# Splitting the shared expert's weights on another engine, and the routing weights and slot experts at other places

## The reference, cut to what matters

```python
xt = x.reshape(-1, 256)                                   # 4096 tokens
scores = softmax(xt @ gate_w.T)                           # 8 experts
_, idx = top_k(scores + gate_bias, 2)
weights = take_along_axis(scores, idx, axis=1)
for e in range(8):
    gate_e = sum(where(idx == e, weights, 0.0), axis=1)
    h = silu(xt @ w1[e].T) * (xt @ w3[e].T)
    y = y + gate_e[:, None] * (h @ w2[e].T)
z = silu(xt @ sw1.T) * (xt @ sw3.T) @ sw2.T               # the shared expert, 512 wide
return y + z
```

## Time and profile before

| | |
|---|---|
| median of 3 timed runs | 662.98 us (662.78 to 662.98) |
| profiled execution, time | 657.85 us |
| its span | 656.1 us |
| PE busy | 556.5 us (85%) |
| DVE busy | 467.4 us (71%) |
| ACT busy | 329.1 us (50%) |
| POOL busy | 269.9 us (41%) |
| granted PE clock, mean | 0.936 |

### The profile page before, as it was taken

One profiled execution on the slowest core, in us unless ns is written; L12 is line 12 of the kernel. 1 busy time (PEld: TensorE's weight loads), 2 busy tenths in 40 slices (PEclk: granted clock), 3 DMA queues, 4 the chain that ended last, 5 costly groups with the idle time before them and its releaser, 6 DMA issues.

```text
span 656.1 us, 11544 instructions
## 1 busy us (share of the span) xinstructions
PE 556.5 (85%) x3488; PEld 484.3 (74%) x3488; DVE 467.4 (71%) x1252; ACT 329.1 (50%) x678; POOL 269.9 (41%) x564
## 2 busy tenths in 40 slices
PE   2728899966598997953799999899999999998885
PEld 1727489956567997632788888688888888887764
DVE  4983997888499874568777764566666666665795
ACT  0516998424389870651455443255555555554321
POOL 4061300033223001000677666366667666665680
PEclk9878999969698998987799999999999999999998
DMA  9998000000000001900222222323333333331994
GB/s 275 335 268 3 1 1 1 2 1 0 1 0 1 2 1 58 400 25 0 73 92 83 83 75 91 98 91 101 106 107 107 107 103 109 100 107 65 316 309 144
DMA packets 57130, 63.04 MB, mean 96 GB/s; under 512 B 14736, under 2 KB 50448, under 8 KB 57072
## 3 DMA queue, kind: packets, MB, share of 16 engines
q1 hardware_dynamic: 49216, 43.75, 23.3%
q0 software_dynamic: 6480, 17.90, 7.7%
q10 hardware_dynamic: 1376, 0.66, 0.5%
HBM read 30.64 MB, written 31.65 MB: 95 GB/s over the span
## 4 chain that ended last, share of the span: by engine, by line
PE 51%; DVE 6%; issue 1%; ACT 1%; POOL 0%; DVEq 0%; POOLq 0%
PE bank L1206 15%; PE bank L1208 15%; PE bank L1207 15%; PE bank L1329 2%; PE bank L1345 2%; PE bank L1214 1%; PE bank L1258 1%; DVE h_lo L1136 1%; DVE XN L975 1%; DVE sw_lo L1021 1%; DVE X L1109 0%; DVE mv L972 0%; DVE X L1119 0%; PE bank L1231 0%; ACT sw_hi L890 0%
## 5 line engine op out<-in xcount | busy, mean ns | idle before, releaser
L830 POOL DMA_INDIRECT slots_in<-X,slot x64 | 68.5, 1070 | 86.4 <-DVEq L1093 52.8
L854 POOL DMA_INDIRECT token_out<-YS,to_row x71 | 71.7, 1010 | 54.3 <-DVE back L1173 50.2
L577 PE MATMUL a_bank<-VO,E_hi 128*128 128x258 f32 x272 | 78.1, 287 | 6.9 <-DVE E_lo L484 6.8
L581 PE MATMUL a_bank<-VO,E_lo 128*128 128x258 f32 x272 | 77.5, 285 | 0.0
L579 PE MATMUL a_bank<-VO,E_hi 128*128 128x256 f32 x272 | 77.4, 285 | 0.0
L1162 DVE TENSOR_TENSOR hr<-bank,sr 128x256 f32<-128x256 f32 x71 | 30.1, 425 | 59.4 <-ACT sr L934 59.4
L1206 PE MATMUL bank<-W_hi,XST_hi 128*128 x142 | 61.8, 435 | 0.5 <-DVE XST_lo L1178 0.5
L934 ACT ACTIVATE sr<-bank 128x256 f32<-128x256 f32 x71 | 27.3, 385 | 63.2 <-PE bank L1208 63.2
L1206 PE MATMUL bank<-XT_hi,sw_hi 128*128 128x512 f32 x128 | 52.1, 407 | 7.7 <-DVE XT_lo L1013 6.1
L577 PEld LDWEIGHTS a_bank<-VO,E_hi 128*128 128x128 f32 x272 | 52.2, 192 | 7.8 <-DVE E_lo L484 7.8
L908 ACT ACTIVATE h_hi<-hf 128x512 fp32r<-128x512 f32 x32 | 20.2, 632 | 74.2 <-DVE hf L1128 74.2
(11 more groups left out here) (241 smaller groups left out, 1700.1 us busy)
## 6 DMA issues: line engine op xcount, KB each, us to landing
XS<-slots_in SPq DMA_DIRECT2D x71, 131.0 KB, 2.0
slots_in<-blank SPq DMA_DIRECT2D x7, 1179.0 KB, 14.4
YG<-token_out SPq DMA_DIRECT2D x16, 512.0 KB, 8.7
W_raw<-in_wT_dram SPq DMA_DIRECT2D x8, 768.0 KB, 13.0
X<-in_x_dram SPq DMA_DIRECT2D x8, 512.0 KB, 7.1
out_dram<-X SPq DMA_DIRECT2D x32, 128.0 KB, 1.9
token_out<-YS,to_row POOLq DMA_INDIRECT x71, 2.5
slots_in<-blank SPq DMA_DIRECT2D x1, 1048.0 KB, 14.7
```

The costliest lines, as they stand in the source:

```text
L577: pe.matmul(O_ps[Q % 2][j][:, 0:D + 2], E_hi[:, n % NE, cols], VO[:, kt, 0:D + 2], start=(kt == 0), stop=False)
L581: mm = pe.matmul(O_ps[Q % 2][j][:, 0:D + 2], E_lo[:, n % NE, cols], VO[:, kt, 0:D + 2], start=False, stop=(kt == qt))
L830: pool.indirect_dma_start(out=xs, out_offset=bass.IndirectOffsetOnAxis(ap=slot[k][:, t:t + 1], axis=0), in_=X[:, t, :], in_offset=None).th ...
L854: pool.indirect_dma_start(out=ys, out_offset=bass.IndirectOffsetOnAxis(ap=to_row[:, i:i + 1], axis=0), in_=YS[:, i % NYS, :], in_offset=No ...
```

## The change

Three things are moved, none is removed.

1. The split of the shared weights goes to POOL, all four instructions, behind its constants and as soon as the two loads have landed. ACT loses L889 to L891, DVE L1019 to L1022. PE waits for the new semaphore `s_slo`.
2. The weights of the two choices (5 instructions of DVE) are worked out behind `chosen` and ahead of the wait for the counts. `s_slot` is now counted by each of the two instructions that write `slot[k]`, with no wait behind the second; the scatters of the first group are issued for choice 0 as soon as `slot[0]` is there, and for choice 1 behind `slot[1]`.
3. `slot_experts()` stands in chunk 4 (`n == MC`) instead of chunk 0. Its count of `s_slot` is waited for as 3.

```diff
@@ gpsimd
+            pool.wait_ge(s_w, 32)
+            for w, (raw, hi, lo) in enumerate(((sw13_raw, sw13_hi, sw13_lo), (sw2_raw, sw2_hi, sw2_lo))):
+                pool.tensor_copy(hi[:, :, :], raw[:, :, :]).then_inc(s_shi, 1)
+                pool.wait_ge(s_shi, w + 1)
+                pool.tensor_tensor(lo[:, :, :], raw[:, :, :], hi[:, :, :].bitcast(f32), ALU.subtract)\
+                    .then_inc(s_slo, 1)
...
             pool.wait_ge(s_slot, 1)
-            for t in range(NT):
-                if t % GT == 0 and t > 0:
+            for t in range(GT):
+                scatter(t, 0)
+            pool.wait_ge(s_slot, 2)
+            for t in range(GT):
+                scatter(t, 1)
+            for t in range(GT, NT):
+                if t % GT == 0:
                     pool.wait_ge(s_sc[t // GT - 1], 16 * TOPK * GT)
                 for k in range(TOPK):
-                    pool.indirect_dma_start(out=xs,
...
+                    scatter(t, k)
...
-            pool.wait_ge(s_slot, 2)
+            pool.wait_ge(s_slot, 3)
@@ scalar
             logits_copy(NG - 1, 1)
-            act.wait_ge(s_w, 32)
-            act.activation(sw13_hi[:, :, :], sw13_raw[:, :, :], ACT.Copy).then_inc(s_whi, 1)
-            act.activation(sw2_hi[:, :, :], sw2_raw[:, :, :], ACT.Copy).then_inc(s_whi, 1)
@@ vector
-            dve.wait_ge(s_whi, 3)
-            for raw, hi, lo in ((sw13_raw, sw13_hi, sw13_lo), (sw2_raw, sw2_hi, sw2_lo)):
-                dve.tensor_tensor(lo[:, :, :], raw[:, :, :], hi[:, :, :].bitcast(f32), ALU.subtract)\
-                   .then_inc(s_wlo, 1)
             group_lo(0)
...
+            for k, out in ((1, X[:, :, W1]), (0, X[:, :, DW])):
+                done(dve.tensor_tensor(tmp[:, :, :], pick[k][:, :, :], score[:, :, :], ALU.mult))
+                done(dve.tensor_reduce(out, tmp[:, :, :], AX.X, ALU.add))
+            done(dve.tensor_tensor(X[:, :, DW], X[:, :, DW], X[:, :, W1], ALU.subtract))
+            dve.wait_ge(s_cols, 3)
             dve.wait_ge(s_cnt, 1)
...
-                done(dve.tensor_copy(slot[k][:, :], red[:, :]))
-            for k, out in ((1, X[:, :, W1]), (0, X[:, :, DW])):
...
-            dve.wait_ge(s_cols, 3)
-            dve.sem_inc(s_slot, 1)
+                dve.tensor_copy(slot[k][:, :], red[:, :]).then_inc(s_slot, 1)
...
-                        if n == 0:
+                        if n == MC:
                             slot_experts()
@@ tensor
-            pe.wait_ge(s_wlo, 3)
+            pe.wait_ge(s_slo, 2)
...
-            pe.wait_ge(s_slot, 2)
+            pe.wait_ge(s_slot, 3)
```

More of the change, by code:

```diff
@@ L697, in attention_and_experts @@
         s_wlo = sem("f_wlo")
+        s_shi = sem("f_shi")
+        s_slo = sem("f_slo")
         s_mv = sem("f_mv")
@@ L823, in _, with scatter @@
                                      pattern=[[1, P]], channel_multiplier=-1))
-            pool.wait_ge(s_slot, 1)
-            for t in range(NT):
-                if t % GT == 0 and t > 0:
+            pool.wait_ge(s_w, 32)
[4 more added lines that the diff above has]
+                    .then_inc(s_slo, 1)
+            def scatter(t, k):
+                pool.indirect_dma_start(out=xs,
+                                        out_offset=bass.IndirectOffsetOnAxis(ap=slot[k][:, t:t + 1], axis=0),
+                                        in_=X[:, t, :], in_offset=None).then_inc(s_sc[t // GT], 16)
+            pool.wait_ge(s_slot, 1)
+            for t in range(GT):
[5 more added lines that the diff above has]
+                if t % GT == 0:
                     pool.wait_ge(s_sc[t // GT - 1], 16 * TOPK * GT)
                 for k in range(TOPK):
-                    pool.indirect_dma_start(out=xs,
-                                            out_offset=bass.IndirectOffsetOnAxis(ap=slot[k][:, t:t + 1], axis=0),
-                                            in_=X[:, t, :], in_offset=None).then_inc(s_sc[t // GT], 16)
+                    scatter(t, k)
             def meta_of(i):
@@ L1086, in _ @@
                 done(dve.tensor_reduce(red[:, :], tmp[:, :, :], AX.X, ALU.add))
-                done(dve.tensor_copy(slot[k][:, :], red[:, :]))
-            for k, out in ((1, X[:, :, W1]), (0, X[:, :, DW])):
-                done(dve.tensor_tensor(tmp[:, :, :], pick[k][:, :, :], score[:, :, :], ALU.mult))
-                done(dve.tensor_reduce(out, tmp[:, :, :], AX.X, ALU.add))
-            done(dve.tensor_tensor(X[:, :, DW], X[:, :, DW], X[:, :, W1], ALU.subtract))
-            dve.wait_ge(s_cols, 3)
-            dve.sem_inc(s_slot, 1)
+                dve.tensor_copy(slot[k][:, :], red[:, :]).then_inc(s_slot, 1)
             def slot_experts():
```

## The result

| | before | after |
|---|---|---|
| median of 11 runs each, side by side | 661.18 us (658.10 to 663.78) | 656.05 us (654.51 to 658.01) |
| ratio of the times, 95% interval | | 0.992 (0.9902 to 0.9939) |
| profiled execution, its span | 657.85, 656.1 | 654.51, 652.8 |

The change is worth 5.1 us by the medians, 5.3 by the ratio (4.0 to 6.5 by its interval); 5.5 were forecast. The two profiled executions differ by 3.3 us only, and a good part of this study is about the gap between these two numbers.

A forecast was written before the change was run, and what follows sets the result against it. DVE was taken as the bound from the end of the logits until PE's outputs(0) at 315.13. Savings 4.4 + 0.9 + 1.3 less 1.1 make 5.5 us: median 662.98 to 657.5 us, range 655.7 to 662.2.

The forecast's parts named there:

- Part 1, saved 4.40 us: End of logits: with the split on POOL, group 0's XT_lo ends at 287.97 instead of 292.37, saving 4.40 us.
- GpSimd's work: Split on POOL: two copies and two subtractions sum to 10.7 us, end near 276, covered because PE needs it at 288.
- What GpSimd holds up: Logits loop: SBUF-only DVE instructions wait for POOL's instruction in flight; both copies into X slip in, nothing paid, 0.97 us slack.
- GpSimd's semaphore wait: Behind POOL's first copy: its subtraction waits for a semaphore, so DVE's second copy into X gets in first.
- Rival A: Logits loop: second DVE copy waits for POOL's subtraction, 4.3 us lost, total 661.8; with B near no change, chance 0.19.
- Rival B: Logits loop: reciprocal and both DVE copies held in turn; 662.9 (chance 0.19 with A), or slower, 667.2 (chance 0.09).
- Part 2, 0.9 us: Choices' weights on DVE ahead of the counts: cost 1.4 us where 2.3 stood, filling 0.67 us idle; saved 0.9.
- Part 3, 1.3 saved, 1.1 given back: slot_experts moved: chunk 0's hf to h_lo falls 2.69 to 1.39 us; PE stalls 1.1 us at outputs(4), cover 0.2.
- Rival C: Chunk 4: PE's wait for L1119 doesn't bite, no stall; 6.6 us saved, 656.4; chance 0.62 together with the forecast.
- Sum: Whole change: 4.4 + 0.9 + 1.3 - 1.1 = 5.5 us saved, with PE's outputs(0) at 308.5.
- TensorE's clock: PE's restart at outputs(0): clock is low after an idle stretch that stays about as long; cost kept, 0.7 us either way.
- What is late next: End of group 5: slot loads behind the last scatter; scatters move by 6.3 us, PE by 5.5, so loads stay in cover.

The follow-up runs named there:

- the further version: Changed kernel with slot_experts in chunk 6 and chunk 0's hf, h_lo ahead of the counts wait; 654.1 and 653.4 us, ratios 0.987 and 0.9917 against the kernel before.
- The extra subtraction: Changed kernel plus an unused GpSimd subtraction (128 x 1536) right behind its first copy, without a wait; 657.97 us, ratio 0.9907 against the kernel before.

## Why the prediction was right, point by point

- **Part 1, saved 4.40 us**: 4.39 in every profile that has the part. `XT_lo` of group 0 ends at 288.21 (287.97 forecast, in a stage that started 0.24 us later).
- **GpSimd's work**: 1.90, 4.59, 1.04 and 2.37 us where 1.94, 5.1, 1.06 and 2.6 were forecast; end at 275.68 (near 276). The copies were right, the subtractions over by a tenth. The estimate by the Trainium skill, GPSIMD Engine Reference, § Performance versus the Vector engine, 4.50 us for 2048 wide, was nearer (measured 4.59).
- **What GpSimd holds up**: the result was right (copies of 1.28 and 0.19 us, nothing paid), the mechanism half so. That a copy of VectorE is held by the instruction in flight holds for subtractions too (2.01 us). That the second got through because of GpSimd's semaphore wait fell: it gets through without one. So the right result rested on a wrong reason here, and that part is luck. Rival A (chance 0.19 together with B) did not come true in any profile; why the copy got through while queued instructions in the earlier trace rows did not stays open. Rival B also fell at its first link: the `reciprocal`, which it had held by GpSimd's first copy, ran inside it in 0.35 us. The reading under both, that VectorE waits with whatever works in SBUF alone, was too wide.
- **Part 2, 0.9 us**: mis-sized by a little. Alone it was 1.26 us: 0.84 for the cover, 0.25 for the waits behind the slot copies, which the sum had not counted, and 0.17 for a shorter `expert`, which part 3 takes away in any case.
- **Part 3, 1.3 saved, 1.1 given back**: 1.40 and 0.97. Rival C, no stall, is refuted in all seven profiles that have `slot_experts` in chunk 4. The step was sound: cover of 0.2 us was read off the rows of TensorE and VectorE there.
- **Sum**: 5.5 forecast; 5.8 by the sections that repeat, 5.3, 5.1 and 3.8 by the ratios. `outputs(0)` at 308.57 for 308.5.
- **TensorE's clock**: "0.7 us either way" was meant for the restart at `outputs(0)`. The step from `outputs(0)` to `outputs(1)` took 6.02 to 7.03 us in the profiles (6.38 in before), so the size was right. It missed a second place of 1.3 us, R to G, which is there without the change too.
- **What is late next**: the prediction saw that the slots' loads stand behind the last scatter, and that both move alike. The scatters started 6.0 us sooner (6.3 forecast), the last one 10.1 us sooner and with it the slots' loads (405.53 instead of 415.65), so that `XSN` still starts straight behind the last addition. It did not say how near the next bound was, which is what held back the further version.

## What to carry to other kernels

When work goes to GpSimd, list VectorE's instructions that work in SBUF alone during that time, and ask for each whether it starts inside one of GpSimd's instructions. A copy that did was held for the rest of that instruction, and only the slack of the loop around it paid for it; the `reciprocal` and the subtractions that read PSUM went on unhindered, so look in the trace for which kinds are held.
A short piece of work moved off the critical path belongs where its engine waits for another one, not merely to a later turn: the same four instructions cost 0.97 us in chunk 4 and 0.12 in chunk 6.
After each cut of the main path compare the start of what it feeds with the chain beside it: here 3.6 us of margin stood before GpSimd's scatters became the bound, and a wait placed four scatters later took nearly 12 of 99.5 us out of their chain.

## What the hardware showed beyond that

- A copy of GpSimd over 128 x 2048 f32 takes 1.90 us and over 1024 wide 1.04, 0.9 to 1.0 ns for an element of each partition; the subtraction of two SBUF operands 4.59 and 2.37, 2.2 to 2.3 ns. The extra subtraction with one tile as both operands took 2.76 us for 1536, 1.8 ns an element.
- The rise of TensorE's clock in the loop over logits came up to 3 us apart in executions of the same instructions, which is 1.3 us of time.
- The medians of the kernel before in the five comparisons were 659.0 to 664.1 us. A gain of 1 us in this kernel is read from sections of the trace; the medians of 4 to 12 runs do not tell it.
